# Linear attention's weights loaded through ScalarE's queue, and their high and low halves shared out otherwise among ScalarE, VectorE and GpSimd

## The reference, cut to what matters

```python
x = x + linear_attention(layernorm(x), Wq, bq, Wk, bk, Wv, bv, Wbeta, bbeta, Walpha, balpha)

q = (x @ Wq + bq).reshape(B, T, H, S)          # 4 heads of 128
k = (x @ Wk + bk).reshape(B, T, H, S)
v = (x @ Wv + bv).reshape(B, T, H, S)
k = k / maximum(norm(k), 1e-12)
alpha_val = sigmoid(x @ Walpha + balpha)
beta = softplus(x @ Wbeta + bbeta)
...                                            # chunks of 128 rows, decayed state
```

## Time and profile before

| | |
|---|---|
| median of 3 runs | 959.72 us (959.37 to 959.97) |
| the profiled execution, its own time | 959.89 us |
| its span in the trace | 958.2 us |
| granted clock of TensorE | 0.999 |
| PE busy | 940.9 us, 98% of the span |
| DVE, ACT, POOL busy | 609.0, 460.3, 479.3 us |

### The profile page before, as it was taken

How to read it: one execution, slowest core, us unless ns; L and a number is a source line. 1 busy time by engine, 2 the same in 40 slices (tenths; PEclk the granted TensorE clock), 3 DMA queues, 4 the chain that set the end, 5 groups by cost and what they waited for, 6 DMA issues and landing times.

```text
span 958.2 us, 13269 instructions
## 1 busy us (share of the span) xinstructions
PE 940.9 (98%) x4725; PEld 534.3 (56%) x4744; DVE 609.0 (64%) x1128; ACT 460.3 (48%) x918; POOL 479.3 (50%) x487
## 2 busy tenths in 40 slices
PE   6999999999999999999999999999999999999998
PEld 4888888888734454444544455445454444544443
DVE  7455656849677576776865466445475676766543
ACT  4443324356577545664433355323454665456630
POOL 5433424377366676666840043304233466665575
PEclk9999999999999999999999999999999999999999
DMA  9401300024210000000000000000000000110001
GB/s 319 167 12 34 132 23 23 1 89 133 89 43 0 1 1 1 1 1 1 1 1 1 1 1 1 1 1 1 1 1 1 1 0 1 45 44 1 1 23 67
DMA packets 14738, 30.31 MB, mean 32 GB/s; under 512 B 2064, under 2 KB 2128, under 8 KB 14672
## 3 DMA queue, kind: packets, MB, share of 16 engines
q1 hardware_dynamic: 14672, 29.45, 8.8%
HBM read 25.22 MB, written 4.23 MB: 31 GB/s over the span
## 4 chain that ended last, share of the span: by engine, by line
PE 91%; DVE 3%; ACT 2%; POOL 1%; issue 1%; DMA 1%; SPq 0%; POOLq 0%; DVEq 0%
PE psum L2066 53%; PE psum L2280 14%; PE psum L2282 13%; PE psum L2408 7%; PE psum L2097 2%; PE psum L2419 1%; DMA wqk_raw<-wk 1%; PE psum L2175 1%; DVE wv_lo L1507 1%; PE psum L2086 1%; ACT probs L1324 0%; DVE xb_lo L1974 0%; ACT xb_hi L1330 0%; POOL hid L865 0%; DVE smax L1966 0%
## 5 line engine op out<-in xcount | busy, mean ns | idle before, releaser
L869 POOL TENSOR_TENSOR hid<-hid,hid_hi 128x512 f32<-128x512 f32 x88 | 102.7, 1167 | 96.5 <-DVE hid_hi L1767 96.5
L2280 PE MATMUL psum<-xf,w_gu 128*128 128x512 f16 x352 | 133.8, 380 | 0.0
L2280 PE MATMUL psum<-xf,w_s 128*128 128x512 f16 x264 | 100.1, 379 | 1.1 <-DVE up L1740 0.5
L2282 PE MATMUL psum<-xf,w_gu 128*128 128x512 f16 x264 | 100.1, 379 | 0.0
L1188 ACT ACTIVATE hid_lo<-hid 128x512 f16<-128x512 f32 x88 | 55.0, 625 | 40.2 <-POOL hid L869 40.2
L865 POOL TENSOR_TENSOR hid<-up,gate 128x512 f32<-128x512 f32 x44 | 56.1, 1274 | 21.7 <-ACT gate L1183 21.7
L2282 PE MATMUL psum<-xq,w_s 128*128 128x512 f16 x176 | 66.7, 379 | 0.0
L2280 PEld LDWEIGHTS psum<-xf,w_gu 128*128 128x128 f16 x352 | 34.3, 97 | 54.1 <-ACT acc L1173 15.5
L1183 ACT ACTIVATE gate<-gate,sg_xs 128x512 f32<-128x512 f32 x44 | 31.7, 721 | 58.7 <-DVE gate L1750 58.6
L731 POOL TENSOR_TENSOR xrstd<-xvar,minus_half 128x1 f32<-128x1 f32 x48 | 25.9, 549 | 65.3 <-DVE xvar L1443 65.3
L1767 DVE TENSOR_SCALAR hid_hi<-hid 128x512 f16<-128x512 f32 x88 | 39.1, 445 | 26.7 <-POOL hid L865 25.1
(11 more groups left out here) (307 smaller groups left out, 2553.2 us busy)
## 6 DMA issues: line engine op xcount, KB each, us to landing
cla_wide<-cla_dram SPq DMA_DIRECT2D x16, 256.0 KB, 3.3
out<-xres SPq DMA_DIRECT2D x16, 256.0 KB, 2.0
xres<-x SPq DMA_DIRECT2D x3, 1024.0 KB, 13.2
codes_gu<-gateT SPq DMA_DIRECT2D x1, 2816.0 KB, 11.5
codes_gu<-upT SPq DMA_DIRECT2D x1, 2816.0 KB, 10.9
codes_da<-downT SPq DMA_DIRECT2D x1, 1536.0 KB, 6.8
codes_db<-downT SPq DMA_DIRECT2D x1, 1280.0 KB, 9.9
xres<-x SPq DMA_DIRECT2D x4, 256.0 KB, 3.4
```

The lines of the kernel that those rows point to most:

```text
L869: nc.gpsimd.tensor_tensor(hid[:, :], hid[:, :], hid_part(hid_hi, j, half), ALU.subtract).then_inc(rest_done, 1)
L2280: nc.tensor.matmul(bank(use[0]), w, x_operand(piece, k, False), start=start and k == 0, stop=False, skip_group_check=not start)
L2282: last = nc.tensor.matmul(bank(use[0]), w, x_operand(piece, k, True), start=False, stop=k == 1, skip_group_check=not start)
```

## The change

Wk, Wv and Wq are issued by ACT, right behind its activation table load, instead of by SP. SP issues the biases directly behind `w_ab`, then waits for Wq to have landed (`wq_in`) and only then issues the other 12 tiles of x. On ACT the high halves of the first three blocks of Wk come first, then `wab`, then the halves of x with the fourth block of Wk between them. On POOL three low blocks of Wk come before `wab`'s, and two low blocks of Wv, which DVE made before, are new. DVE makes two low blocks of Wv instead of four.

```diff
@@ sync
             sp.dma_start(raw[:, :, 0:2 * AB], w_ab.rearrange("(k p) n -> p k n", p=P)).then_inc(wab_in, 16)
-            weights(wqk_raw[:, KT * D:2 * KT * D], wk, wk_in)
-            weights(wv_raw[:, :], wv, wv_in)
-            weights(wqk_raw[:, 0:KT * D], wq, wq_in)
             sp.dma_start(bk_rows[:, :], bk.partition_broadcast(P)).then_inc(rows_in, 16)
...
             sp.dma_start(bq_col[:, :], bq).then_inc(rows_in, 16)
+
+            sp.wait_ge(wq_in, 16)
             for g in range(1, 4):
                 sp.dma_start(xs[g], xv[g]).then_inc(x_rest_in, 16)
@@ gpsimd
-            pool.wait_ge(wa_hi, 1)
+            def weight_low(lo, raw, hi, k, n, done):
+                pool.wait_ge(wa_hi, n)
+                nc.gpsimd.tensor_tensor(cols(lo, k), cols(raw, k), cols(hi, k).bitcast(F32),
+                                        ALU.subtract).then_inc(done, 1)
+
+            for k in range(KT - 1):
+                weight_low(wqk_lo, wqk_raw, wqk_hi, KT + k, 1 + k, wk_lo_done)
+            pool.wait_ge(wa_hi, 4)
             low, raw = (w[:, :].rearrange("p (k n) -> p k n", k=KT)[:, :, AB:2 * AB] for w in (wab, wab_raw))
             nc.gpsimd.tensor_tensor(low, raw, low.bitcast(F32), ALU.subtract).then_inc(wab_lo_done, 1)
-
-            for w0, ks, hi0, done in ((KT, range(KT - 1), 2, wk_lo_done), (0, range(2, KT), 2 * KT, wq_lo_done)):
-                for k in ks:
-                    pool.wait_ge(wa_hi, hi0 + k)
-                    nc.gpsimd.tensor_tensor(cols(wqk_lo, w0 + k), cols(wqk_raw, w0 + k),
-                                            cols(wqk_hi, w0 + k).bitcast(F32), ALU.subtract).then_inc(done, 1)
+            for k in (2, 3):
+                weight_low(wv_lo, wv_raw, wv_hi, k, 6 + k, wv_lo_done)
+            for k in (2, 3):
+                weight_low(wqk_lo, wqk_raw, wqk_hi, k, 8 + k, wq_lo_done)
@@ scalar
             nc.scalar.preload_act_table_set("natural_log_exp_and_others")
-            act.wait_ge(wab_in, 16)
-            nc.scalar.activation(wab[:, :], wab_raw[:, :], ACT.Copy).then_inc(wa_hi, 1)
+            for dst, src, loaded in ((wqk_raw[:, KT * D:2 * KT * D], wk, wk_in), (wv_raw[:, :], wv, wv_in),
+                                     (wqk_raw[:, 0:KT * D], wq, wq_in)):
+                act.dma_start(dst.rearrange("p (k n) -> p k n", k=KT),
+                              src.rearrange("(k p) n -> p k n", p=P)).then_inc(loaded, 16)
...
+            for k in range(3):
+                weight_hi(wk_in, wqk_hi, wqk_raw, KT + k)
+            act.wait_ge(wab_in, 16)
+            nc.scalar.activation(wab[:, :], wab_raw[:, :], ACT.Copy).then_inc(wa_hi, 1)
             split_hi("start", 0, 0)
             split_hi("start", 0, 1)
-            weight_hi(wk_in, wqk_hi, wqk_raw, KT)
+            weight_hi(wk_in, wqk_hi, wqk_raw, KT + 3)
             split_hi("start", 0, 2)
             split_hi("start", 0, 3)
-            weight_hi(wk_in, wqk_hi, wqk_raw, KT + 1)
-            weight_hi(wk_in, wqk_hi, wqk_raw, KT + 2)
-            weight_hi(wk_in, wqk_hi, wqk_raw, KT + 3)
@@ vector
-            for k in range(KT):
+            for k in range(2):
                 dve.wait_ge(wa_hi, 2 + KT + k)
                 nc.vector.tensor_tensor(cols(wv_lo, k), cols(wv_raw, k), cols(wv_hi, k).bitcast(F32),
                                         ALU.subtract).then_inc(wv_lo_done, 1)
```

## The result

The changed kernel takes 966.06 us in the median of 5 runs (965.68 to 966.64), the kernel before, measured beside it, 959.97 us (5 runs): a ratio of 1.0065, 95% interval 1.0054 to 1.0075. The forecast was 960.6 (958.8 to 961.9), "within 0.2%". The profiled execution of the changed kernel has a span of 964.3 us against 958.2.

What follows compares the result with a forecast made beforehand. PE, busy 98% of the span, was taken as the bound, so only Q's start counts: +2.7 us (logits later) - 1.8 (three waits gone) = +0.9, giving 960.6 us, range 958.8 to 961.9.

Steps and rivals of the forecast that it cites:

- Step 1: Transfers at the start: Wk and x share the bus evenly and both land at 9.9 us.
- t: Landing time of Wk: 10.71 us before the change, forecast 9.9.
- u: Landing time of x's fourth tile: about 6.8 us before the change, forecast 9.9.
- The rivals: Bus faster with two queues (959.3 or 958.2 us, chance 0.30); late ACT issue (961.4, 0.13); clock falls (961.5, 0.15); no effect.
- Wk by 8.5: Sign of being wrong: Wk lands by 8.5 us, where 9.5 to 10.5 was expected.
- x by 7.5: Sign of being wrong: x's fourth tile still lands by 7.5 us, so the queues don't share evenly.
- Step 1's two small terms: Landings 0.4 us sooner from ACT's issue near 0.85, and 0.4 us from 551 small packets moving behind x.
- Step 2: ACT's halves of x now stand behind Wk's high halves: logits start at 16.2 instead of 13.53, 2.7 us later.
- Step 3: Logits to V: three waits of PE go, 1.8 us given back, leaving 5.2 us; V to Q stays 2.86.
- Step 4: Low halves on DVE and POOL: counted in pairs of 1.71 us, ready just before Q; cost nothing, or up to 0.5 us.
- Step 5: SP issues x's other rows at 17.0 us; they land at about 26.3, before DVE wants them at 27.31: no cost.
- The clock: Rival: PE idles before x's transposes, its clock falls to 1.2 GHz, 0.9 us more, 961.5 us; chance 0.15.

Runs made afterwards that it cites:

- e4: The changed kernel with Wk alone issued by ACT; SP issues Wv and Wq behind w_ab and doesn't wait: 963.14 us.
- e1: The changed kernel's order and shares of halves, with SP issuing all transfers in the old order: 964.21 us, ratio 1.0042 to the kernel before.
- e10: e1 with 24 instead of 6 warming matmuls behind the transposes, which kept the clock at full level: 961.99 us.
- e11: The changed kernel with ACT issuing its three weights only after SP has issued x's four tiles: 965.16 us.
- e12: The changed kernel with SP issuing w_ab ahead of x's four tiles: 967.14 us.
- e6: The changed kernel with POOL making w_ab's low half first and Wk's low halves only behind the fourth normalisation: 966.53 us.
- e5: The changed kernel with 30 instead of 10 warming matmuls ahead of the transposes: 966.04 us.
- e8: The kernel before, with POOL starting Wq's low halves only behind DVE's four of Wv: 959.9 us, ratio 1.0001.
- e13: The changed kernel with two more instructions, unread semaphore increments, on DVE ahead of its first normalisation: 965.10 us.
- e2: The kernel before with ACT issuing Wk, Wv and Wq and SP waiting for Wq, its order of halves kept: 965.91 us, ratio 1.0064.
- e3: The changed kernel with ACT waiting until x's fourth tile has landed before it issues Wk, Wv and Wq: 967.57 us.

## Why the prediction was wrong

- **Step 1, the transfers: the step that failed.** "I take an even share: both land together" gave t = u = 9.9. Measured: t = 6.6, u = 11.9. Wk's transfer, 0.46 us ahead in issue, had 438 of its 512 packets moved before the first of x (2.6 of the 5.1 us by e4); behind that x shared the bus with Wv and Wq (2.5). The 2.0 us of u alone take the forecast from 960.6 to 962.6, past its range. The rivals varied how fast the sum of bytes arrives, never which queue is served first, although the step itself says "whichever is favoured". x was the side without slack, and Wk had landed 5.3 us before it. Of the prediction's signs of being wrong "Wk by 8.5" came; "x by 7.5" names the opposite case, in which x is favoured.
- **Not that step alone.** With all transfers as before, the order of halves still gives 964.21 (e1), outside the range as well. Of its 4.4 us the clock is 2.2 by the medians (e10), and DVE's shorter stream 0.7. With the clock kept, steps 2 and 3 come out: Q at 24.54, against 24.9 from the prediction's sums with e1's landings.
- **Step 1's two small terms.** ACT's issue at 0.81 during the table load was right, and here that head start did harm: without it (e11) the kernel is 0.9 us faster. The 0.4 us for the 551 small packets had the right sign: with w_ab's in front again (e12) x is 1.25 us later. Their price, w_ab at 14.9, is worth 0.1 us by the same run.
- **Step 2, ACT and the halves of x.** The order was right; its size was u + 6.3 to the logits and came out as u + 8.0. Of the 1.7, 0.7 is the fourth normalisation, which took 1.45 instead of 0.54 us beside POOL's low halves (e6). "Hidden" in the step looked only at their end and not at what they do to DVE meanwhile. ACT's first half of x also came 3.5 instead of 2.4 us behind u, behind w_ab (14.90), and the transposes ran at a clock of 0.50; but w_ab early (e12) and the clock kept (e5) each give back only 0.1 at the logits, alone. How the remaining 1.0 divides stays open.
- **Step 3, what is given back.** 5.2 us from logits to V against 5.1 measured: right. V to Q took 3.3 instead of 2.9.
- **Step 4, the low halves.** That DVE and POOL run in turn was right: from 20.15 to 27.55 us, 7.4 us, against 6.8 for the pairs. "Cost nothing; if the cover is missing, up to 0.5 us" was short of what stands behind them: `kn`, 0.7 us, on which Q's bank depends. It cost 0.3 us here, and it limits the kernel before as well (e8).
- **Step 5, the other rows of x.** They landed 8.5 us behind their issue and no wait for them is on PE: right.
- **The clock.** The mechanism of the rival came (0.50 from 12.2 to 19.0 us), its price did not: 0 in this kernel (e5), 0.9 to 2.2 us where PE is the one that is late (e1 to e10). The Trainium skill (TensorE: Matmul & The Clock Gate, Why this matters for your kernels) warns against idle gaps of TensorE between bursts of matmuls. The rows agree: PE stood from 8.5 to 13.6 us, and its granted clock fell to 0.50 at 12.2. The runs add that the fall costs nothing where DVE's chain ends later than PE's.
- **Not foreseen.** Some 0.7 us from a shorter instruction stream on DVE (e13): the edit touches only the start of the program and still lengthens two stalls far behind it. Left unexplained: 0.3 us of the shift that appear behind 916 us.

In sum: 5.1 (x) + 1.3 (behind x) - 1.4 (given back) + 0.7 (DVE's stream) + 0.3 (open) = 6.0, against 6.1 measured. These are parts of one path, not what each gives back when taken away alone: with x as early as before (e11) the kernel is still 5.3 us over, and the order of halves alone costs 4.4 (e1).

## What to carry to other kernels

In these runs a transfer that was issued first went nearly whole before the first packet of the other queue, and only then was the bus shared. So the transfer that has no slack is issued first, and a large one that may wait is cut or issued later. Look as well at which transfers then share the bus with it. When a wait of PE for one tile is to be removed, look at what stands behind that tile on the same engine: here the next one was late by almost the same time. Filling TensorE's idle time with warming matmuls paid where TensorE itself was late (e10), and gave nothing where DVE was (e5).

## What the runs showed of the hardware

- **Two queues.** First nearly all that one queue had been given before the other's first issue (438 of 512 packets of Wk, 118 of 128 of its first quarter, 476 of x's 512), then both. From 11 to 14 us they move as many packets of 64 bytes as of 2 KB (531 to 526). That isn't so everywhere: in e12, from 5 to 6.5 us, it is 534 to 179. The Trainium skill (DMA: Bandwidth & Descriptors, Issuing engines are not separate DMA queues) says that such transfers interleave and that a second issuer saves only issue time. No kernel got faster by the queue here. But the transfers interleaved only behind the first one, and by that rule nothing would have been lost, where e2 lost 6.1 us.
- **An issue during a table load.** ACT's DMA instruction went out at 0.81 us while its table load ran from 0.78 to 2.06.
- **A place in an instruction stream.** Two more semaphore increments at the start of DVE's stream shorten a stall near 120 us and one near 916 us by some 0.35 us each (e13). In all the kernels with two instructions fewer on DVE both stalls are that much longer. Why isn't shown.
- **A straggler.** In e3 Wk's last engine finished at 14.6 us, the next to last at 13.2.
